# Routed expert rows: scattered into a region per expert and loaded as plain tiles, in place of a token list and row gathers

## The chip, the cores and the metric

The kernel runs on one NeuronCore of a Trainium2 chip. Its engines are TensorE (PE), VectorE (DVE), ScalarE (ACT), GpSimd (POOL) and SyncE (SP); 16 DMA engines move data between HBM and the on-chip SBUF. The metric is the time of one execution on the device, in microseconds, as a median of several runs.

## The reference

The tokens are 16 batches of 128 rows, 2048 in all, of 256 floats. Four blocks with a residual follow each other: a convolution block, a low-rank expert layer, a cross attention, and a mixture of experts. All but the last are computed per batch and aren't touched. The last one:

```python
logits = flat @ router_w.T                      # 2048 x 32
scores = jnp.sqrt(jax.nn.softplus(logits))
_, idx = jax.lax.top_k(scores + expert_bias, 4)
topv = jnp.take_along_axis(scores, idx, axis=1)
topv = topv / (topv.sum(axis=-1, keepdims=True) + 1e-20)
out = sum(p_e[:, None] * swiglu(flat, wg_e, wu_e, wd_e) for e in range(32)) + swiglu(flat, shared...)
x = x + out
```

Each token goes to 4 of 32 experts; an expert has an inner width of 128, and gate and up are clipped to [-7, 7].

## The kernel before

The five engines have one program each, written out by hand. Up to the routed experts the order on an engine is set by a table of ticks: for each engine and kind of step the tick of the first instance (T_PE, T_DVE, T_ACT, T_POOL), and the program goes through all ticks and emits what is due. A batch comes every 128 ticks; a tick has no time of its own, it only orders an engine's instructions. Engines wait for each other by semaphores.

The normalized rows of a batch (xnD, ScalarE) are written by SyncE to the HBM tensor xn_rows (L1367). Routing is done in five groups of batches. For each group VectorE ranks the tokens of every expert and computes a key per token and rank (the four picks of a token, k = 0 to 3, sorted by expert number). GpSimd then scatters the token's number into token_list in HBM, one indirect DMA of 128 pieces of 4 bytes for each batch and rank, 64 in all (L1310); the list has 2048 places for each expert.

Behind the ticks, when the shared expert's 16 steps are done, the list is turned into tiles of 128 rows: SyncE loads it (L1392), TensorE transposes it and selects with one-hot matrices (L552 to L563), VectorE builds those (L925 to L951). The result is idg, the token numbers of 95 tiles (the most that 8192 picks on 32 experts can need), and regs, each tile's weight address. GpSimd gathers the rows of each tile from xn_rows by indirect DMA (L1322) into 32 buffers xg.

The tile loop is a software pipeline of NT + 6 steps. In step t TensorE makes the down product of tile t-5 (L580, out of bank y), transposes tile t (L594, L595), transposes the activated tile t-4 (L598) and makes gate and up of tile t-1 (L606, with weight addresses from registers that it loads for 16 tiles at a time). ScalarE copies the transposed rows (L1222), takes the tanh (L1217) and copies the result into one of four buffers y (L1227). VectorE clips, multiplies and copies (L972, L974, L984, L980), and computes beside it each token's places in y_rows and its weights pk4. SyncE writes each result tile to y_rows (L1396) and counts those that have landed in s_st.

At the end the results are gathered back by token: for each rank, from 3 to 0, and each batch one indirect DMA on GpSimd (L1340) into the same ring xg, then one multiply-add on VectorE into xs (L1062), then the output is written (L1403). A rank's gathers wait for s_st to reach the last tile with such a pick (register thr). y_rows is filled with zeros at the start (L1361), since places without a token may be read.

## Time and profile before

| | us |
|---|---|
| median of 3 runs | 824.38 (823.39 to 824.93) |
| the profiled execution | 827.63 |
| its span, first to last instruction | 825.8 |

| engine | busy us | share |
|---|---|---|
| TensorE matmuls | 608.2 | 74% |
| VectorE | 508.2 | 62% |
| GpSimd | 443.7 | 54% |
| ScalarE | 357.4 | 43% |

The mean granted clock of TensorE is 0.868. Times in the profile are counted from the first instruction. An idle time has behind its arrow what ended it by the trace; "issue" means that the profile shows nothing that the engine waited for, and "remote" an update for which it has no source.

### The profile page before, as it was taken

How to read it: one execution, taken by the hardware profiler on the slowest of the kernel's cores; microseconds unless marked ns; L12 is line 12 of the kernel's file. 1: busy time of each engine (PE TensorE's matmuls, PEld its weight loads, DVE VectorE, ACT ScalarE, POOL GpSimd, SP SyncE). 2: the span in 40 equal slices, each digit the busy share in tenths (PEclk: the TensorE clock that was granted, in tenths of full speed). 3: DMA queues.
4: the chain of work that ended last, by engine and by line, in shares of the span. 5: the costliest groups of instructions: out<-in, count | busy, mean ns of one | idle time of the engine just before them, and what ended most of it. 6: DMA issues, size and time to landing. Idle time of an engine off the chain costs nothing.

```text
span 825.8 us, 13944 instructions
## 1 busy us (share of the span) xinstructions
PE 608.2 (74%) x4063; PEld 485.0 (59%) x4063; DVE 508.2 (62%) x1582; ACT 357.4 (43%) x1012; POOL 443.7 (54%) x592
## 2 busy tenths in 40 slices
PE   0779999999799996998787347741689999678200
PEld 0678777878678785786564136631467777456100
DVE  1537767677976679756773545610388788546733
ACT  1012566567465674657955423210245544334100
POOL 6687573646437885226412473177355552535675
PEclk9999999999799997999877556875699999989655
DMA  7893000000000000007302070033244443335236
GB/s 289 309 349 111 1 8 8 1 8 8 8 8 1 9 8 7 8 2 267 129 7 84 1 273 14 8 113 103 89 138 153 154 145 116 108 96 152 65 108 180
DMA packets 51386, 75.29 MB, mean 91 GB/s; under 512 B 7249, under 2 KB 40529, under 8 KB 51057
## 3 DMA queue, kind: packets, MB, share of 16 engines
q1 hardware_dynamic: 41552, 53.25, 18.4%
q0 software_dynamic: 9760, 21.15, 9.3%
q8 instruction: 35, 0.57, 0.3%
q14 instruction: 39, 0.31, 0.1%
HBM read 44.98 MB, written 29.39 MB: 90 GB/s over the span
## 4 chain that ended last, share of the span: by engine, by line
PE 57%; DVE 15%; issue 11%; another core or an unknown queue 6%; ACT 5%; POOL 3%; DMA 2%; SPq 1%; POOLq 0%; ACTq 0%; DVEq 0%
PE pc L542 10%; PE ps L606 9%; PE pS L580 5%; PE pS L522 4%; PE ps L508 3%; PE ps L338 3%; PE po L493 2%; POOL work L1340 2%; PE ps L378 2%; PE ps L365 2%; PE ps L382 2%; PE ps L399 1%; PE ps L391 1%; DMA arena<-in_ctxT 1%
## 5 line engine op out<-in xcount | busy, mean ns | idle before, releaser
L1322 POOL DMA_INDIRECT work<-xn_rows,tk x95 | 92.1, 969 | 88.3 <-issue 39.7
L542 PE MATMUL pc<-arena,tk 128*128 128x128 f32 x768 | 105.5, 291 | 15.2 <-POOL arena L1298 9.3
L542 PEld LDWEIGHTS pc<-arena,tk 128*128 128x128 f32 x768 | 98.6, 205 | 18.2 <-issue 9.7
L580 PE MATMUL pS<-arena,tk 128*128 x190 | 65.4, 427 | 55.7 <-issue 40.6
L606 PE MATMUL ps<-arena,work 128*128 x380 | 103.8, 398 | 0.0
L1340 POOL DMA_INDIRECT work<-y_rows,tk x64 | 71.0, 1110 | 59.0 <-PE pc L595 24.9
L1298 POOL TENSOR_TENSOR arena<-arena 128x512 f32<-128x512 f32 x64 | 90.1, 1426 | 12.4 <-ACT arena L1097 12.3
L1217 ACT ACTIVATE tk<-work 128x128 f32<-128x128 f32 x95 | 29.4, 309 | 120.4 <-DVE work L972 81.9
L580 PEld LDWEIGHTS pS<-arena,tk 128*128 128x128 f32 x190 | 29.8, 196 | 80.4 <-issue 80.1
L1162 ACT ACTIVATE work<-pS,work 128x128 f32<-128x128 f32 x256 | 72.7, 373 | 7.8 <-DVE work L787 7.7
L1310 POOL DMA_INDIRECT token_list<-pk,ixl x64 | 63.8, 996 | 22.3 <-issue 15.2
L972 DVE TENSOR_SCALAR work<-ps 128x256 f32<-128x256 f32 x95 | 40.1, 422 | 53.4 <-remote 25.0
L606 PEld LDWEIGHTS ps<-arena,work 128*128 128x128 f32 x380 | 68.6, 201 | 5.9
L1235 POOL TENSOR_TENSOR stD<-stD,epsc 128x1 f32<-128x1 f32 x16 | 3.0, 187 | 106.7 <-DVE stD L619 106.7
L787 DVE TENSOR_REDUCE work<-pS 128x4 f32<-128x512 f32 x64 | 43.8, 685 | 26.5 <-PE pS L522 26.5
L769 DVE TENSOR_TENSOR arena<-pc,arena 128x512 f32<-128x512 f32 x64 | 43.8, 684 | 24.6 <-PE pc L542 24.2
L980 DVE COPY tk<-po 128x128 f32<-128x128 f32 x95 | 27.5, 289 | 43.5 <-issue 16.8
L508 PE MATMUL ps<-pk,work 128*128 128x128 f32 x256 | 44.5, 301 | 8.4 <-ACT work L1162 4.6
L1154 ACT ACTIVATE work<-ps 128x512 f32<-128x512 f32 x64 | 37.8, 591 | 23.0 <-PE ps L508 21.5
L1062 DVE SCALAR_TENSOR_TENSOR xs<-work,pk,xs 128x256 f32<-128x256 f32 x64 | 28.1, 478 | 26.6 <-DMA work<-y_rows,tk 24.0
L522 PE MATMUL pS<-arena,work 32*128 32x256 f32 x256 | 40.0, 433 | 0.3
L508 PEld LDWEIGHTS ps<-pk,work 128*128 128x128 f32 x256 | 30.6, 152 | 16.1 <-issue 15.5
(288 smaller groups left out, 1443.7 us busy)
## 6 DMA issues: line engine op xcount, KB each, us to landing
arena<-in_w SPq DMA_DIRECT2D x8, 1536.0 KB
y_rows<-lg SPq DMA_DIRECT2D x1, 12160.0 KB, 38.6
y_rows<-tk SPq DMA_DIRECT2D x95, 128.0 KB
tk<-in_tk SPq DMA_DIRECT2D x1, 2048.0 KB, 10.9
xn_rows<-xnD SPq DMA_DIRECT2D x16, 128.0 KB
out<-xs SPq DMA_DIRECT2D x16, 128.0 KB
pk<-in_pack SPq DMA_DIRECT2D x1, 1588.0 KB, 11.6
xs<-in_x SPq DMA_DIRECT2D x3, 512.0 KB, 11.6
```

Source lines behind the costliest of these rows:

```text
L508: i = pe.transpose(p[:, 128 * k:128 * k + 128], Pt[m % 3][:, 128 * k:128 * k + 128], ident)
L522: i = pe.matmul(p[:, 256 * c:256 * c + 256], qT[b % 3][r, 128 * c:128 * c + 128], kz[b % 3][r, c, :, :].rearrange("p a b -> p (a b)"), sta ...
L542: i = pe.matmul(pv, tk[:, h, 128 * d:128 * d + 128], kvv[:, ci, :, :].rearrange("p b (i h j) -> p (b i) h j", i=8, h=8)[:, :, hl, :], star ...
L580: pe.matmul(p[:, 0:256], hT[n % 2], arena[:, 512:][:, bass.ds(base.pop(n), 256)], start=True, stop=True).then_inc(s_yp, 1)
L606: i = pe.matmul(p[:, 0:256], xgT[n % 3][:, 128 * c:128 * c + 128], arena[:, 256 * c:][:, bass.ds(base[n], 256)], start=(c == 0), stop=(c = ...
L769: dve.tensor_tensor(zv, cbanks.place["conv", n][:, :].rearrange("p (k h j) -> p k h j", h=4, j=8), x1, ALU.mult).then_inc(s_z, 1)
L787: dve.tensor_reduce(mx[:, g, :], sbanks.place["S", m][:, :].rearrange("p (k m) -> p k m", k=4), AX.X, ALU.max, negate=True).then_inc(s_mx, 1)
L1162: i = act.activation(Pt[m % 3][:, 128 * k:128 * k + 128], sbanks.place["S", m][:, 128 * k:128 * k + 128], ACT.Exp, bias=mx[:, g, k:k + 1])
L1298: pool.tensor_tensor(kv[kk % 4][:, c, half, :].rearrange("p (i h j) -> p i h j", h=8, i=8), i0, i1, ALU.mult).then_inc(s_kv, 1)
L1310: pool.indirect_dma_start(out=Ld, out_offset=bass.IndirectOffsetOnAxis(ap=ixl[:, b, k:k + 1], axis=0), in_=P("tok")[:, b:b + 1], in_offset ...
L1322: pool.indirect_dma_start(out=xg[n % NX], out_offset=None, in_=Xd, in_offset=bass.IndirectOffsetOnAxis(ap=idg[:, n:n + 1], axis=0)).then_i ...
L1340: pool.indirect_dma_start(out=xg[n % NX], out_offset=None, in_=Yd, in_offset=bass.IndirectOffsetOnAxis(ap=ixy[:, b, k:k + 1], axis=0)).the ...
```

## The change

The regions that the token list had become regions of rows. The key of a pick, minus one, is now directly a row of the HBM tensor expert_rows, with 2048 rows for each expert and 512 more, each 272 floats: 256 of data, then the number of its place in y_rows. At the start SyncE writes the places' numbers into xn_rows, which now has four copies of each token (one per rank), and fills all 32 regions with padding rows, whose place is one of 512 dump rows. ScalarE writes the normalized rows, four copies, and takes over SyncE's weight and row loads. For each batch and rank SyncE loads 128 rows into one of four staging buffers, and GpSimd scatters them by the key.

The list load, its transposes and selections go. A tile is a plain load of 128 rows from an address in a register (12 buffers in place of 32, four loads in flight), computed from the experts' counts in a few small steps beside the shared expert (ta to te). GpSimd scatters each result tile to y_rows by the places that came with the rows, and the results are read back as plain loads of four batches at a time into four buffers of their own. The weight extraction in the loop moves from step 44 to step 6 on, the threshold computation changes. The ticks have new values throughout; those of GpSimd and the new ones of SyncE are shown.

```diff
-NT = 95
+U = 128
+Q = 128 // U
+NT = -(-((NB * 128 * KT + NE * (U - 1)) // U) // Q)
+ROW = 272
-NX = 32
+DUMP = 512
+NX = 12
-        xg = [carve([128, 256]) for _ in range(NX)]
+        xg = [carve([128, 260]) for _ in range(NX)]
+        rb = [carve([128, 4, 256]) for _ in range(4)]
-        T_POOL = {"rsA": 70, "rsB": 680, "rsC": 818, "rsD": 1153, "vc": 269, "us": 405, "kv": 279, "xb": 699,
-            "xc": 1050, "list": 1914}
+        T_POOL = {"rsA": 84, "rsB": 684, "rsC": 812, "rsD": 1148, "vc": 297, "us": 337, "kv": 273, "xb": 801,
+            "xc": 1117, "list": 1899}
+        T_SP = {"fill": 1162, "st": 1855}
...
@@ tensor_program, the tile loop
-                    pe.wait_ge(d_g[n % 8], 16 * (n // 8 + 1))
+                    pe.wait_ge(d_g[n % 4], 16 * Q * (n // 4 + 1))
@@ vector_program, the end
-                dve.scalar_tensor_tensor(out=xs[:, b, :], in0=xg[n % NX], scalar=pk4[:, b, k:k + 1], in1=xs[:, b, :],
-                                         op0=ALU.mult, op1=ALU.add).then_inc(s_fin, 1)
+            for m in range(4 * KT):
+                g, k = m % 4, KT - 1 - m // 4
+                dve.wait_ge(d_r[g], 16 * (m // 4 + 1))
+                for i in range(4):
+                    b = 4 * g + i
...
+                    dve.scalar_tensor_tensor(out=xs[:, b, :], in0=rb[g][:, i, :], scalar=pk4[:, b, k:k + 1], in1=xs[:, b, :],
+                                             op0=ALU.mult, op1=ALU.add).then_inc(s_fin, 1)
@@ scalar_program
+                for b in at(t, T_ACT["xd"], 128, NB):
+                    act.wait_ge(s_xn["D"], b + 1)
+                    act.dma_start(Xd[:, 128 * b:128 * b + 128, 0:256].rearrange("k p d -> p k d"),
+                                  xnD[b % 2][:, :].unsqueeze(1).broadcast_to((128, KT, 256))).then_inc(d_xn[b % 2], 16)
@@ gpsimd_program
+                        j = KT * b + k
                         pool.wait_ge(s_ixl, g + 1)
+                        pool.wait_ge(d_st[j % 4], 16 * (j // 4 + 1))
                         pool.indirect_dma_start(
-                            out=Ld, out_offset=bass.IndirectOffsetOnAxis(ap=ixl[:, b, k:k + 1], axis=0),
-                            in_=P("tok")[:, b:b + 1], in_offset=None).then_inc(d_list, 16)
...
+                            out=Xs, out_offset=bass.IndirectOffsetOnAxis(ap=ixl[:, b, k:k + 1], axis=0),
+                            in_=stage[:, j % 4, :], in_offset=None).then_inc(d_list[j % 4], 16)
+
+            for n in range(NT + 3):
+                if n >= 3:
+                    pool.wait_ge(d_y[(n - 3) % 4], 16 * ((n - 3) // 4 + 1))
+                    pool.sem_inc(s_st, 1)
+                if n < NT:
+                    pool.wait_ge(s_y, n + 1)
+                    pool.indirect_dma_start(
+                        out=Yr, out_offset=bass.IndirectOffsetOnAxis(ap=xg[n % NX][:, 256:257].bitcast(U32), axis=0),
+                        in_=y[n % 4], in_offset=None).then_inc(d_y[n % 4], 16)
@@ sync_program
+            for t in range(TICKS):
+                for e in (*at(t, 0, 1, 14), *(14 + n for n in at(t, T_SP["fill"], 36, NE - 14))):
+                    sp.dma_start(Xs[e * NB * 128:(e + 1) * NB * 128, :].rearrange("(j p) d -> p j d", p=128),
+                                 stage[:, e % 4, :].unsqueeze(1).broadcast_to((128, NB, ROW))).then_inc(d_zero, 16)
...
+                        if j == 0:
+                            sp.wait_ge(d_zero, 16 * (NE + 2))
+                        if k == 0:
+                            sp.wait_ge(d_xn[b % 2], 16 * (b // 2 + 1))
+                        if j >= 4:
+                            sp.wait_ge(d_list[j % 4], 16 * (j // 4))
+                        sp.dma_start(stage[:, j % 4, :], Xd[k, 128 * b:128 * b + 128, :]).then_inc(d_st[j % 4], 16)
+            sp.wait_ge(s_regs, 1)
...
+                if n >= 4:
+                    sp.wait_ge(d_g[n % 4], 16 * Q * (n // 4))
+                if n >= NX:
+                    sp.wait_ge(d_y[(n - NX) % 4], 16 * ((n - NX) // 4 + 1))
+                for k in range(Q):
+                    r = sp.snap(half[Q * n % WR + k], min_val=0, max_val=NE * NB * 128 + 384)
+                    sp.dma_start(xg[n % NX][U * k:U * k + U, :], Xs[bass.ds(r, U), 0:260]).then_inc(d_g[n % 4], 16)
...
+            for m in range(4 * KT):
+                g, k = m % 4, KT - 1 - m // 4
+                if g == 0:
+                    sp.wait_ge(s_st, last[k])
+                    sp.sem_inc(s_thr, 1)
+                if m >= 4:
+                    sp.wait_ge(s_fin, 4 * (m - 4) + 4)
+                o = DUMP + NB * 128 * k + 512 * g
+                sp.dma_start(rb[g], Yr[o:o + 512, :].rearrange("(b p) d -> p b d", p=128)).then_inc(d_r[g], 16)
```

Three places show the order of instructions. First SyncE from the last input loads on, before (lg is a block of zeros, xnD the normalized rows, in_w the experts' weights):

```order
L1361 DMA y_rows<-lg 128x95x256
L1367 DMA xn_rows<-xnD 128x256 x11
L1378 DMA arena<-in_w 128x4x768 x5
L1367 DMA xn_rows<-xnD 128x256 x3
L1370 DMA tk<-in_w 128x768
```

And after (in_dest holds the places' numbers, in_pad the padding rows):

```order
L1339 DMA xn_rows<-in_dest 8192x16
L1341 DMA stage<-in_pad 128x1088
L1343 DMA expert_rows<-stage 128x4x272
L1347 DMA expert_rows<-stage 128x16x272 x32
L1359 DMA stage<-xn_rows 128x272 x64
```

The writes of rows and the loads of weights have left SyncE's queue, and 64 staging loads stand behind 32 region fills.

Second GpSimd, where the first group's scatters begin. After (st... are the statistics of the layer norms, L1296 the products for the convolution):

```order
L1303 TENSOR_TENSOR xs<-xs,rows 128x256
L1296 TENSOR_TENSOR arena<-arena 128x512
L1310 DMA expert_rows<-stage,ixl 66048x272
L1296 TENSOR_TENSOR arena<-arena 128x512
L1310 DMA expert_rows<-stage,ixl 66048x272
L1236 TENSOR_TENSOR stD<-stD,epsc 128x1
L1238 TENSOR_TENSOR stD<-stD,nhalf 128x1
L1240 TENSOR_SCALAR stD<-stD 128x1
```

The scatters stand among the statistics and the products, as the list scatters did, but each now stands behind a wait for its staging load.

Third the end of GpSimd's program, before:

```order
L1235 TENSOR_TENSOR stD<-stD,epsc 128x1
L1237 TENSOR_TENSOR stD<-stD,nhalf 128x1
L1239 TENSOR_SCALAR stD<-stD 128x1
L1310 DMA token_list<-pk,ixl 65536x1 x23
L1322 DMA work<-xn_rows,tk 128x256 x95
L1328 TENSOR_LOAD thr
L1329 ISA
L1340 DMA work<-y_rows,tk 128x256 x64
```

And after:

```order
L1236 TENSOR_TENSOR stD<-stD,epsc 128x1
L1238 TENSOR_TENSOR stD<-stD,nhalf 128x1
L1240 TENSOR_SCALAR stD<-stD 128x1
L1310 DMA expert_rows<-stage,ixl 66048x272 x22
L1320 DMA y_rows<-tk,work 8704x256 x95
```

Both sets of gathers, 95 and 64, are gone from GpSimd, and 95 scatters of results have come.

## Rows read from the trace of the kernel before

**Rows 1.** Stages: busy time and count of each engine, clock, DMA share.
```profile
core 0: us, PE busy (x) PEld busy (x) DVE busy (x) ACT busy (x) POOL busy (x), PEclk, DMA share, GB/s
...
60.00:380.00 320.00, 295.76 (x2365) 245.27 (x2364) 232.80 (x660) 187.50 (x519) 181.18 (x286) 0.97 0.05 16
...
528.00:590.00 62.00, 20.28 (x74) 14.47 (x73) 11.16 (x43) 6.19 (x19) 37.65 (x40) 0.61 0.29 87
590.00:708.00 118.00, 114.36 (x589) 88.27 (x588) 94.49 (x336) 57.45 (x195) 54.44 (x56) 0.99 0.44 136
708.00:770.00 62.00, 45.51 (x216) 34.03 (x214) 31.71 (x111) 21.51 (x72) 30.34 (x32) 0.92 0.41 124
770.00:825.80 55.80, 0.04 (x1) 0.00 (x0) 27.10 (x62) 0.38 (x1) 40.69 (x32) 0.51 0.41 117
```

**Rows 2.** Timeline of GpSimd, 533 to 582: start, duration, operation, idle before.
```profile
533.75 0.98 POOL L1322 DMA_INDIRECT work<-xn_rows,tk  x1 [23.78 <-DVE tk L949]
535.04 0.96 POOL L1322 DMA_INDIRECT work<-xn_rows,tk  x1 [0.30 <-issue]
...
581.36 0.95 POOL L1322 DMA_INDIRECT work<-xn_rows,tk  x1 [0.30 <-issue]
```

**Rows 3.** Timeline of ScalarE: copies of transposed tiles 0, 6, 8 and later.
```profile
537.30 0.38 ACT L1222 ACTIVATE work<-ps 128x256 f32<-128x256 f32 x1 [8.52 <-PE ps L595]
...
577.39 0.38 ACT L1222 ACTIVATE work<-ps 128x256 f32<-128x256 f32 x1 [10.39 <-remote]
...
590.99 0.38 ACT L1222 ACTIVATE work<-ps 128x256 f32<-128x256 f32 x1 [0.89 <-PE ps L595]
...
597.32 0.36 ACT L1222 ACTIVATE work<-pc 128x256 f32<-128x256 f32 x1
...
598.98 0.36 ACT L1222 ACTIVATE work<-ps 128x256 f32<-128x256 f32 x1
...
633.51 0.36 ACT L1222 ACTIVATE work<-pc 128x256 f32<-128x256 f32 x1
...
635.82 0.38 ACT L1222 ACTIVATE work<-ps 128x256 f32<-128x256 f32 x1 [0.55 <-PE ps L595]
...
712.60 0.36 ACT L1222 ACTIVATE work<-pc 128x256 f32<-128x256 f32 x1
...
762.87 0.36 ACT L1222 ACTIVATE work<-ps 128x256 f32<-128x256 f32 x1
```

**Rows 4.** Timeline of TensorE in the first tiles of the loop.
```profile
558.11 1.22 PE L580 MATMUL pS<-arena,tk 128*128 x2 [10.28 <-issue]
...
582.14 1.22 PE L580 MATMUL pS<-arena,tk 128*128 x2 [20.47 <-issue]
```

**Rows 5.** Waits, 484 to 500 us: total, times, longest.
```profile
ACT pk L1184 <- remote: 9.7, 1, 9.7
```

**Rows 6.** Timelines of VectorE and GpSimd in the tail.
```profile
769.02 13.56 DVE L1062 SCALAR_TENSOR_TENSOR xs<-work,pk,xs 128x256 f32<-128x256 f32 x34
...
823.21 0.48 DVE L1062 SCALAR_TENSOR_TENSOR xs<-work,pk,xs 128x256 f32<-128x256 f32 x1 [0.94 <-DMA work<-y_rows,tk]
...
773.01 10.39 POOL L1340 DMA_INDIRECT work<-y_rows,tk  x1 [0.30 <-DVE xs L1062]
```

**Rows 7.** Stages again: y_rows written in 1 KB rows, then weights read.
```profile
45.00:50.00 5.00, 3.97 (x32) 3.72 (x32) 1.21 (x3) 0.60 (x1) 4.90 (x6) 1.00 1.05 348
382.00:396.00 14.00, 11.44 (x95) 8.17 (x92) 10.17 (x33) 11.39 (x35) 9.90 (x14) 1.00 1.03 403
```

**Rows 8.** The list tensor: durations min/median/max in ns, first and last start.
```profile
L1310 POOL DMA_INDIRECT token_list<-pk,ixl x64: 954/976/1113, 264.2 to 508.9; - x64
```

**Rows 9.** VectorE, TensorE and the chain between shared expert and first tile.
```profile
528.09 0.17 DVE L631 TENSOR_SCALAR tk<-cum 128x32 f32<-128x32 f32 x1
...
536.57 0.48 PE L594 MATMUL ps<-pk,work 128*128 128x128 f32 x1 [2.37 <-DMA work<-xn_rows,tk]
...
535.04 2.67 DMA work<-xn_rows,tk
```

424 lines of the change are left out of this document (177 added, 247 removed), and 9 rows, old and new, of tables (T_ACT, T_DVE, T_PE).

## The prediction

> **What bounds the kernel now.** I read the stages first: busy time of each engine from 60 us on [rows 1]. Until 380 us TensorE is busy 295.76 of 320 us and the DMA engines 5%: a compute stage with an almost idle memory side. From 590 to 708 us, the plain run of the expert tiles, TensorE is busy 114.36 of 118 us. Between and behind them lie three stretches where nothing is busy that should be: 528 to 590 (TensorE 20.28 of 62 us), 708 to 770 (45.51 of 62) and 770 to the end (none of 55.8 us).
>
> The first hole begins when GpSimd starts its row gathers. They go out back to back, one each 1.25 us (533.75, 535.04, ... 581.36), because 32 tile buffers are free [rows 2]. The loop advances only slowly meanwhile: ScalarE copies the transposed rows of tile 0 at 537.30, of tile 6 at 577.39, of tile 8 at 590.99 [rows 3]. TensorE stands still for 10.28 and 20.47 us "by issue", with no DMA named [rows 4]. Once GpSimd is throttled by the buffers, one gather per tile, the loop runs: tile 8 at 590.99, tile 74 at 712.60 are 1.84 us a tile, and a plain step, 597.32 to 598.98, is 1.66 us [rows 3]. The same pattern stands at the other bursts: while 16 list scatters leave back to back, ScalarE waits 9.7 us for an update no row accounts for [rows 5]. I read this as: a long back-to-back burst of indirect DMAs on GpSimd delays the updates TensorE sends to others. The trace shows the coincidence, not the cause.
>
> The tail: VectorE is through the loop at 769.02, runs 34 accumulations in 13.56 us, and the remaining ones come at the pace of GpSimd's gathers until 823.21; the span ends at 825.8 [rows 6].
>
> **Part by part; the sum is made on the profiled execution** (827.63 us, span 825.8), whose time lies 3.25 us above the median of the three runs; differences are applied to that median, 824.38.
>
> *Fill of the regions.* SyncE writes 32 regions of 2048 rows of 1088 B, 71.3 MB, from SBUF, where the kernel before writes 12.45 MB. Plain writes of 1024 B rows ran at 348 GB/s with all DMA engines busy (1.05), and descriptors of 3 KB at 403 GB/s [rows 7]. Per row that is 46.8 ns and 122 ns of an engine, so about 9 ns fixed and 0.037 ns per byte; 1088 B take 49.1 ns, and 65,536 of them on 16 engines 201 us. The fill can start when the loads are through and the pad rows sit in SBUF, at 38 to 47 us by my estimate (loads of 8.7 MB at 300 to 400 GB/s, then 8192 pieces of 64 B for the token numbers). During it ScalarE issues seven or eight fourfold writes of the normalized rows, 0.5 MB each, some 1.5 us of all engines apiece: 11 us. So it ends between 250 and 260 us, or about 280 if the token numbers take long or an odd row size costs a little. The cover is the compute stage, DMA share 0.05 [rows 1]. Who waits: SyncE holds the first staging load until all fills have landed, GpSimd's first scatter waits for that load, and behind it in GpSimd's order stand the rstd steps and the products for the convolution, for which TensorE waits. The first list scatter of before left at 264.2 us [rows 8]; a staging load needs some 2.7 us [rows 9]. So a loss of 0 to 20 us; I take +5.
>
> *Scatter of rows instead of a list.* 64 scatters on GpSimd either way, 1 us each. Now each needs a staging load through four buffers. A round of load (about 2.7 us), scatter (1 us) and landing (2.7 us) is 6.4 us per four, 1.6 us each in place of 1.26. At the end 22 stand in a row, 35 us from 474: through at 509 to 515, and they are needed only when the shared expert is done at 528. Covered; without that cover it would be some 8 us. What a late staging load costs GpSimd's other work in the compute stage is bounded by one round, 0 to 6 us, and I count it inside the +5.
>
> *Index tables.* Out goes the chain list load, transposes, two selections, gather: from 528.09 on VectorE to the first transposed tile at 536.57, 8.5 us [rows 9]. In come some 25 small VectorE operations of 0.17 to 0.2 us beside the shared expert, where VectorE is nearly the bound: +4.5. Behind the last shared step remain two transposes, two casts, a register load, one DMA: 0.5+0.5+0.65+0.3+2.7 = 4.7 us, -3.8; the register load is read off the step at 633.51, which has one on TensorE and lasts 2.31 us for 1.66 [rows 3]. Together +0.7.
>
> *The loop.* Gathers leave GpSimd, plain loads on SyncE take their place (12 buffers, four in flight); GpSimd now scatters each result, one per tile, at 0.95 to 1.25 us under a step of at least 1.66. It can never burst: each scatter waits for its own result. So the hole from 528 to 590 should go, and with it the burst at 709 and its hole. ScalarE's copies of tile 0 and tile 94 are 225.6 us apart now (537.30, 762.87) [rows 3]. 94 steps cost 156 us at the plain step and 173 at 1.84; the one-hot work of before on 512-wide tiles in the loop is dropped, the weight extraction stays, so I take 1.78, 167.3 us: -58.3. The reuse of a tile buffer closes in time: result of tile n written at step n+5, scatter and landing some 4 us, load 3 us, is under ten steps of twelve.
>
> *The tail.* 64 gathers become 16 loads of 512 KB that do not wait for tile buffers. Of the 95 tiles 79 hold tokens in these inputs, and the four ranks are complete after tile 67, 74, 77 and 79 (counted from the reference's routing), so all are ready before the loop ends; but only four read buffers exist, so most of the reading runs beside VectorE. 64 accumulations at 13.56/34 = 0.40 us are 25.6 us, +2 for late loads (512 KB at 348 GB/s 1.5 us against 1.6 us of work per group), +2.6 for the last output (823.21 to 825.8), +2 for GpSimd to drain: 32 us, where 56.8 stand now [rows 6]: -24.8. Bounds: 28 with perfect reads, 56.8 if reading is as slow as gathers.
>
> What GpSimd does under VectorE's run is visible: the gather issued at 773.01 took 10.39 us, not 0.95, while VectorE ran its 34 accumulations [rows 6]. The last two or three scatters of the new loop meet 64 of them; they carry padding tiles, so no read waits for them, only the end of the program does. The Trainium skill, "SBUF — State Buffer", section on who interferes with whom, says that VectorE and GpSimd share a port pair as an exclusive lock and that descriptor writing on GpSimd starves meanwhile, and asks for the plain queues; the trace agrees in kind. By that rule the drain would come wholly after VectorE's last operation, 3 x 1.25 + 2.7 = 6.5 us instead of 2.6+2, a sum 2 us higher.
>
> **Sum:** +5 +0.7 -58.3 -24.8 = -77.4; 824.4 - 77.4 = **747 us**.
>
> **Rivals.** *The fill is late.* The rows are 1088 B, a multiple of 64 but not of the usual powers, while the price above is from 1024 B rows. If each costs 56 ns, the fill takes 230 us, ends at 290 and GpSimd is held 20 to 40 us in the compute stage: about 775. For it: the estimate ends within 10 us of the need, and nothing in the trace has such a row. Against: even 280 costs little. The Trainium skill, "DMA: Bandwidth & Descriptors", section "How a descriptor splits into AXI transactions", states that a piece not starting on 256 B is split further and fetches unused bytes: up to 40 beats in place of 34, which gives the 56 ns by the same fit; no row here shows it. Chance 0.17.
>
> *The holes stay.* If the silence of TensorE's updates hangs on something other than the burst (say, on any indirect DMA beside it at the loop's start), 40 to 50 us of the gain fail: about 793. Against: from 590 to 708 GpSimd issues one per tile and nothing stalls [rows 1, 3]. 0.12.
>
> *Slower than before.* The loop's step becomes the scatter's. GpSimd allows three result scatters in flight and waits for the one three tiles back before it issues the next; four result buffers stand behind ScalarE's copy. If a 128-row scatter to HBM needs L us to land beside the tile loads, the step is about (L+1)/3. From 1.78 to 2.6 us a tile costs 94 x 0.82 = 77 us and eats all the gain; that needs L of 7 us, against 2.67 for a gather [rows 9]. At 3 us a tile: 860 us. 0.05.
>
> *Better than that.* The paced row scatters no longer hold up the routing stage, where 9.7 us and some smaller waits sit on the chain [rows 5]: about 733. 0.2.
>
> **How the numbers follow.** My forecast has 0.46 (735 to 762), the better case 0.2, the late fill 0.17, the holes 0.12, slower 0.05. To leave out no more than two in ten the range goes from 722 (better case with clean steps of 1.66 us) to 788 (late fill with all of its 40 us). A change of under 0.2%, some 1.6 us, is about what this measurement cannot tell from none; hardly any case ends there. Faster 0.94, same 0.01, slower 0.05.
>
> **What would show it.** Right: DMA share near 1 from about 40 to 250 us with the convolution running at its old pace; GpSimd's first row scatter near 265; no idle TensorE of over 3 us inside the loop; 1.7 to 1.85 us between ScalarE's copies throughout; VectorE's 64 accumulations in under 30 us, end 3 to 7 us later. Wrong: GpSimd waiting at its first scatter well past 275 while TensorE idles; TensorE idle "by issue" near the first tiles; ScalarE's copy of a result waiting for the scatter's landing; VectorE waiting for each read group.

## The result, and the profile after

The changed kernel takes **782.29 us** (median of 4 runs, 781.09 to 783.03), the kernel before 824.52 in the same comparison; the ratio is 0.9488 (95% interval 0.9472 to 0.9505). The forecast was 747, range 722 to 788: right in direction and inside the range, but the gain is 42.2 us and not 77.4. A second measurement of the same kernel, beside e9, gave 777.98 us (e10), so some 4 us lie between comparisons.

The profiled execution has a span of 781.2 us (before 825.8). The DMA row of its page, in 40 slices of 19.5 us:

```profile
DMA  8999999999999433101343924952344343434669
```

It stands at 8 or 9 up to the 13th slice, 254 us: the fill. Stages, with the columns of [rows 1]:

```profile
core 0: us, PE busy (x) PEld busy (x) DVE busy (x) ACT busy (x) POOL busy (x), PEclk, DMA share, GB/s
60.00:380.00 320.00, 286.14 (x2286) 237.63 (x2286) 237.39 (x632) 182.64 (x499) 174.24 (x274) 0.96 0.74 236
528.00:554.00 26.00, 2.78 (x13) 1.51 (x11) 2.76 (x10) 0.79 (x3) 6.73 (x7) 0.59 0.27 83
554.00:743.00 189.00, 170.09 (x835) 133.36 (x834) 123.19 (x433) 81.75 (x277) 85.90 (x88) 0.93 0.44 134
743.00:781.20 38.20, 5.28 (x22) 3.04 (x20) 29.29 (x77) 2.98 (x10) 10.87 (x7) 0.61 0.80 264
```

Against [rows 1], the long standstill at the loop's start is gone, and so is the slow tail. But from 528 to 554 TensorE is again busy for only 2.78 us, before the loop has begun, and inside the loop it is idle for 19 us, of which no forecast of mine had more than a few.

**Where the loop starts.** The timeline of SyncE's queue and of ScalarE, and the total of GpSimd's row scatters (durations min/median/max in ns, first and last start; then what it waited for):

```profile
550.88 7.12 SPq L1376 DMA_DIRECT2D work<-expert_rows  x12
```

```profile
553.83 0.38 ACT L1223 ACTIVATE work<-ps 128x256 f32<-128x256 f32 x1 [24.97 <-PE ps L593]
```

```profile
L1310 POOL DMA_INDIRECT expert_rows<-stage,ixl x64: 957/963/1192, 267.9 to 548.2; - x64
its engine sat idle before it (us, times) until:
  DMA stage<-xn_rows: 41.8, 11
```

Tile 0 is copied at 553.83, where [rows 3] had 537.30 and the forecast comes to 543. The first tile load waits for the last scatter, issued at 548.2 and not at 509 to 515. GpSimd waited 41.8 us for its four staging buffers to be loaded. The last scatters, in its timeline:

```profile
528.48 0.96 POOL L1310 DMA_INDIRECT expert_rows<-stage,ixl  x1 [6.28 <-DMA stage<-xn_rows]
529.75 0.96 POOL L1310 DMA_INDIRECT expert_rows<-stage,ixl  x1 [0.30 <-issue]
535.03 0.96 POOL L1310 DMA_INDIRECT expert_rows<-stage,ixl  x1 [4.33 <-DMA stage<-xn_rows]
536.30 0.96 POOL L1310 DMA_INDIRECT expert_rows<-stage,ixl  x1 [0.31 <-issue]
541.63 0.96 POOL L1310 DMA_INDIRECT expert_rows<-stage,ixl  x1 [4.37 <-DMA stage<-xn_rows]
```

They come in pairs, 6.6 us apart: 3.3 us a scatter, where I had put 1.6. SyncE issues the last staging loads in pairs too:

```profile
532.18 0.80 SPq L1359 DMA_DIRECT2D stage<-xn_rows  x2
538.73 0.79 SPq L1359 DMA_DIRECT2D stage<-xn_rows  x2
545.34 0.32 SPq L1359 DMA_DIRECT2D stage<-xn_rows  x1
```

Each of these stands 2.4 us behind the second scatter of a pair (529.75, 536.30, 542.89), at its landing. The reason is the order. The buffer of scatter j is j % 4. Group 3 (batches 12 to 14) has 12 scatters at ticks 16 apart from 1408 on, group 4 (batch 15) four from 1536 on, so the last four of group 3 and the four of group 4 stand at the same ticks, and both engines take them in turn: 56, 60, 57, 61, 58, 62, 59, 63. Their buffers are 0, 0, 1, 1, 2, 2, 3, 3. Every second load needs the buffer of the scatter just ahead of it and waits for that scatter to land.

**Inside the loop.** Copies of tiles 15, 16 and 17 on ScalarE, and TensorE between the first two:

```profile
579.03 0.37 ACT L1223 ACTIVATE work<-pc 128x256 f32<-128x256 f32 x1
584.10 0.38 ACT L1223 ACTIVATE work<-ps 128x256 f32<-128x256 f32 x1 [3.68 <-PE ps L593]
587.09 0.38 ACT L1223 ACTIVATE work<-pc 128x256 f32<-128x256 f32 x1 [0.44 <-PE pc L593]
```

```profile
583.09 0.69 PE L577 MATMUL pS<-arena,tk 128*128 x2 [3.61 <-issue]
```

Most steps take 1.66 us or alternate between 1.47 and 2.10. The steps into tile 16, 32, 48, 64 and 80 take 5.07, 5.07, 5.90, 5.96 and 5.43, and each of them is followed by one of 2.6 to 3.2. These are the places at which TensorE loads 16 registers with expert bases. The loads, in before and in after:

```profile
L572 PEldq TENSOR_LOAD <-regs x6: 1257/1313/1789, 534.5 to 733.2; - x6
```

```profile
L568 PEldq TENSOR_LOAD <-regs x6: 4112/4298/4533, 531.0 to 712.1; - x6
L1366 SPq TENSOR_LOAD <-regs x6: 977/1170/1481, 545.7 to 705.4; - x6
```

The same 16 words cost TensorE 1.31 us before and 4.30 after, while SyncE loads 16 words of the same row in 1.17 (medians).

**The tail** is as forecast; VectorE from the end of the loop on:

```profile
749.48 8.00 DVE L1040 SCALAR_TENSOR_TENSOR xs<-work,pk,xs 128x256 f32<-128x256 f32 x20
757.79 16.29 DVE L1040 SCALAR_TENSOR_TENSOR xs<-work,pk,xs 128x256 f32<-128x256 f32 x40 [0.32 <-DMA work<-y_rows]
775.41 1.67 DVE L1040 SCALAR_TENSOR_TENSOR xs<-work,pk,xs 128x256 f32<-128x256 f32 x4 [1.33 <-DMA work<-y_rows]
```

64 accumulations are through at 777.1; from 749.3 to the span's end are 31.9 us, against 32 forecast and 56.8 before [rows 6].

The account of the two spans, measured between ScalarE's copies of tile 0 and tile 94 (742.91): start +16.5, loop 189.1 in place of 225.6 = -36.5, from tile 94 to the end 38.3 in place of 62.9 = -24.6; together -44.6. That is the difference of the two profiled spans; the medians differ by 42.2.

### The profile page after: what moved, and what is told of

Read it like the earlier page. It is cut to its first block, busy times and chain, and to the rows that moved or that the text cites. A ratio compares the mean times of both kernels' runs of the same rounds, so it can differ in the third digit from the quotient of the medians.

```text
span 781.2 us, 14111 instructions
## 1 busy us (share of the span) xinstructions
PE 600.9 (77%) x4045; PEld 480.6 (62%) x4045; DVE 511.7 (65%) x1554; ACT 356.5 (46%) x1010; POOL 376.5 (48%) x526
## 4 chain that ended last, share of the span: by engine, by line
PE 31%; SPq 29%; DMA 14%; issue 10%; DVE 8%; POOL 4%; ACT 3%; ACTq 0%; DVEq 0%; POOLq 0%
SPq L1347 26%; PE ps L605 8%; PE pS L577 5%; DMA stage<-xn_rows 3%; DMA expert_rows<-stage,ixl 3%; DMA expert_rows<-stage 3%; PE pc L556 2%; POOL y_rows L1320 2%; DMA stage<-in_pad 2%; DMA y_rows<-tk,work 2%; SPq L1330 2%; DVE xs L1040 2%; PE ps L522 2%; PE pS L536 2%; DMA work<-y_rows 1%
## 5 line engine op out<-in xcount | busy, mean ns | idle before, releaser
L1320 POOL DMA_INDIRECT y_rows<-tk,work x95 | 96.8, 1019 | 112.4 <-ACT tk L1228 95.0
L556 PEld LDWEIGHTS pc<-arena,tk 128*128 128x128 f32 x768 | 97.6, 203 | 19.8 <-DVE arena L773 13.3
L1296 POOL TENSOR_TENSOR arena<-arena 128x512 f32<-128x512 f32 x64 | 89.8, 1420 | 11.1 <-ACT arena L1101 11.0
L1310 POOL DMA_INDIRECT expert_rows<-stage,ixl x64 | 63.9, 998 | 59.0 <-DMA stage<-xn_rows 41.8
L1223 ACT ACTIVATE work<-ps 128x256 f32<-128x256 f32 x48 | 17.9, 373 | 45.9 <-PE ps L593 44.5
L1228 ACT ACTIVATE tk<-pS 128x256 f32<-128x256 f32 x95 | 35.8, 377 | 5.0 <-DMA y_rows<-tk,work 5.0
L536 PE MATMUL pS<-arena,work 32*128 32x256 f32 x256 | 37.2, 408 | 0.7 <-ACT work L1151 0.7
## 6 DMA issues: line engine op xcount, KB each, us to landing
arena<-in_w ACTq DMA_DIRECT2D x8, 1536.0 KB, 13.3
```

Source lines behind the costliest of these rows:

```text
L536: i = pe.matmul(p[:, 256 * c:256 * c + 256], qT[b % 3][r, 128 * c:128 * c + 128], kz[b % 3][r, c, :, :].rearrange("p a b -> p (a b)"), sta ...
L556: i = pe.matmul(pv, tk[:, h, 128 * d:128 * d + 128], kvv[:, ci, :, :].rearrange("p b (i h j) -> p (b i) h j", i=8, h=8)[:, :, hl, :], star ...
L1296: pool.tensor_tensor(kv[kk % 4][:, c, half, :].rearrange("p (i h j) -> p i h j", h=8, i=8), i0, i1, ALU.mult).then_inc(s_kv, 1)
L1310: pool.indirect_dma_start(out=Xs, out_offset=bass.IndirectOffsetOnAxis(ap=ixl[:, b, k:k + 1], axis=0), in_=stage[:, j % 4, :], in_offset=N ...
L1320: pool.indirect_dma_start(out=Yr, out_offset=bass.IndirectOffsetOnAxis(ap=xg[n % NX][:, 256:257].bitcast(U32), axis=0), in_=y[n % 4], in_o ...
```

## The experiments

There were five comparisons; e1 to e4, e5 to e8, e9 to e11 and e12 ran on four different chips. The kernel before took 824.5 us in the first comparison, 822.5 beside e1 to e4, 749.8 beside e5 to e8, 822.8 beside e9 to e11 and 749.3 beside e12. Program and inputs are the same in all; what the chip changes is the subject of e5 and e9 to e11. After itself was measured in the first comparison (782.3) and in e10 (778.0) only, so a gain given below against 782.3 could be up to 4 us smaller.

### The register table's place (e1, e2, e7)

In before the table is one row of 96 words, and TensorE loads 16 from each multiple of 16. In after it is 190 words: 95 row addresses for SyncE, then 95 bases for TensorE, so that TensorE's groups start at word 95 + 16 m, 60 bytes behind a multiple of 64 bytes. (Offsets here are counted from the start of the row; where the row itself lies in SBUF is not on record.) e1 changes that:

```diff
-        regs = sb("regs", [1, 2 * Q * NT], I32)
+        regs = sb("regs", [1, 192], I32)
-                    pe.load(half[:w], regs[0:1, Q * (NT + t):Q * (NT + t) + w])
+                    pe.load(half[:w], regs[0:1, 96 + t:96 + t + w])
```

(VectorE's two copies into the table go to words 0 and 96 accordingly. What lies behind the table in SBUF moves by 8 bytes.)

> The changed kernel with nothing altered but where the second half of the register table lies: the expert bases that TensorE loads start at word 96 of the table's row instead of word 95, so that each group of 16 starts at a multiple of 64 bytes again, as it did in the kernel before. In the trace of after TensorE's load of 16 registers takes 4298 ns, in that of before 1313 ns, and the step from tile 15 to 16 (and 31 to 32, 47 to 48, 63 to 64, 79 to 80) takes 5.1 to 5.9 us where a plain one takes 1.66. Theory (the misaligned start makes the load slow): the load is back at 1.2 to 1.8 us, the five steps fall to some 2.3 us, and with the steps at the lower clock behind them 15 to 22 us go: 760 to 767 us. Rival (SyncE's load of its own 16 registers from the same row at about the same time gets in the way): both loads still fall together, TensorE's stays at 4.1 to 4.5 us and the time within 1 us of after's 782.3.

Measured: **754.55 us**, 0.9161 of before (0.9127 to 0.9195). The register loads of e1:

```profile
L568 PEldq TENSOR_LOAD <-regs x6: 1104/1284/1598, 526.9 to 686.3; - x6
L1366 SPq TENSOR_LOAD <-regs x6: 977/1166/1554, 541.4 to 679.4; - x6
```

TensorE's load is fast, and the rival is out. It was a weak one: in both kernels SyncE's second load stands over 7 us ahead of TensorE's (570.2 and 577.9 in after, 566.1 and 573.5 in e1), so they never ran at the same time. The step into tile 16 is 1.84 us (from 574.67) and the one behind it 2.10:

```profile
576.51 0.39 ACT L1223 ACTIVATE work<-ps 128x256 f32<-128x256 f32 x1 [0.45 <-PE ps L593]
578.61 0.37 ACT L1223 ACTIVATE work<-pc 128x256 f32<-128x256 f32 x1
```

The loop's 94 steps take 163.5 us instead of 189.1. That is 25.6 us for one word of padding (23.4 against the 186.9 of e10), more than the 15 to 22 expected: a load of 4.3 us costs the step it stands in 3 to 4 us and the next ones 1 to 2 more. Behind the idle stretch of after the granted clock is down, as the stages (TensorE alone) from 578 us show, its column being the one behind the count:

```profile
578.00:583.00 5.00, 1.48 (x9) 1.00 0.50 158
583.00:587.00 4.00, 3.91 (x14) 0.64 0.20 66
```

e2 makes the opposite edit in the kernel before:

```diff
-        regs = sb("regs", [1, 96], I32)
+        regs = sb("regs", [1, 127], I32)[:, 31:127]
```

> The kernel before, with its register table moved by 31 words, so that each group of 16 registers that TensorE loads starts 60 bytes behind a multiple of 64, as in the changed kernel; SyncE loads nothing there. Theory (alignment): the load goes from 1.31 to 4.1 to 4.5 us, five of them stand in the loop, each adds 3 us and some steps at the lower clock: 838 to 845 us instead of 824.5. Rival (two engines loading at once): one engine loads alone here, 1.3 us each, 824 to 825.5 us.

Measured: 843.95 us, 1.0233 (1.0182 to 1.0284), with one engine loading, as expected; its loop takes 241.7 us where that of before takes 225.6:

```profile
L572 PEldq TENSOR_LOAD <-regs x6: 3938/4176/4302, 532.6 to 747.8; - x6
```

e7 exchanges the two halves in after, so that SyncE has the odd start:

```diff
-                    pe.load(half[:w], regs[0:1, Q * (NT + t):Q * (NT + t) + w])
+                    pe.load(half[:w], regs[0:1, t:t + w])
-                    sp.load(half[:w], regs[0:1, Q * n:Q * n + w])
+                    sp.load(half[:w], regs[0:1, NT + n:NT + n + w])
```

(VectorE's two copies change places accordingly, and SyncE waits for both. The table keeps its 190 words, so nothing else in SBUF moves.)

> The changed kernel with the two halves of the register table exchanged: TensorE's expert bases lie at word 0 (each 16 at a multiple of 64 bytes), SyncE's row addresses at word 95 (60 bytes behind one). Theory (alignment decides, whichever engine loads): SyncE's load goes from 1.17 to about 4 us, TensorE's from 4.3 to 1.3; SyncE issues its loads up to 12 tiles ahead, so its 3 us are covered, and the time is near that of the aligned table, 752 to 758 us. Rival (only TensorE's load suffers from the odd start): SyncE's load stays at 1.0 to 1.5 us, same time.

Measured: 756.36 us (one run). The loads of e7:

```profile
L568 PEldq TENSOR_LOAD <-regs x6: 1219/1383/1633, 529.2 to 690.0; - x6
L1366 SPq TENSOR_LOAD <-regs x6: 3442/3806/3908, 545.1 to 683.0; - x6
```

The slow load follows the odd start to SyncE, and its 3.8 us cost nothing there, since SyncE issues tile loads well ahead. The loop takes 163.5 us again. So the start in the row decides, on either engine. Only an offset of 60 bytes was tried; which offsets are slow is open. The Trainium skill, "Runtime: NRT & Kernel Launch", section "Instruction fetch mechanics", puts register loads at about 200 ns a register, for loads that by the same page come from HBM; for 16 that would be 3.2 us, an estimate. The loads here come from SBUF, and these traces have 82 ns a register at an aligned start (1313/16) and 269 at the odd one, so one figure doesn't cover them.

### The ring of staging buffers (e3, e4, e8, e12)

e3 has eight staging buffers from the 37th scatter on. One of the four new ones is a fifth slice of the old tile; the others are the tiles that held the normalised rows of three earlier stages, free since 444 us:

```diff
+        slots = [stage[:, i, :] for i in range(5)] + [xnABC[:, i, :] for i in range(3)]
+        slot = [j % 4 if j < 36 else j % 8 for j in range(KT * NB)]
+        turn = [slot[:j].count(slot[j]) for j in range(KT * NB)]
...
-                        if j >= 4:
-                            sp.wait_ge(d_list[j % 4], 16 * (j // 4))
-                        sp.dma_start(stage[:, j % 4, :], Xd[k, 128 * b:128 * b + 128, :]).then_inc(d_st[j % 4], 16)
+                        s, c = left[slot[j]]
+                        if turn[j]:
+                            sp.wait_ge(s, c + 16 * turn[j])
...
+                        sp.dma_start(slots[slot[j]], Xd[k, 128 * b:128 * b + 128, :]).then_inc(loaded[slot[j]][0], 16)
```

> The changed kernel with eight buffers for the rows on their way to the scatters instead of four, from the 37th scatter on (a fifth buffer, and the three tiles of normalised rows of earlier stages, free by then). Nothing else moves; the scatters and loads are the same 64 and 64. Theory (the ring of four sets the pace: a load waits for the scatter four places before it, 4.4 us of landing and 2 to 7 us of load for each round): the last 18 scatters go at 1.3 to 1.7 us each instead of 3.2, the last one by 518 to 528 us instead of 548.2, the first tile's copy by 530 to 536 instead of 553.8, and the time falls by 17 to 23 us: 759 to 765 us. Rival (the expert weights that land in the same stretch slow every transfer, so more of them at once only wait longer): the scatters' pace stays above 2.5 us, 776 to 782 us.

Measured: 763.98 us, 0.9284 (0.9247 to 0.9322), as the theory had it. The scatters of e3:

```profile
L1315 POOL DMA_INDIRECT expert_rows<-stage,ixl x52: 956/985/1225, 268.3 to 525.6; - x52
L1315 POOL DMA_INDIRECT expert_rows<-xnABC,ixl x12: 956/959/966, 472.6 to 526.8; - x12
```

The last of all is issued at 526.85 instead of 548.20. The pace was not quite the expected 1.3 to 1.7 us: the last 15 scatters (from 498.14) stand 2.05 us apart on average, the last seven (from 518.97) 1.3.

This edit changes two things at once. There are twice the buffers, and with j % 8 the last eight scatters, 56, 60, 57, 61 and so on, have the buffers 0, 4, 1, 5, 2, 6, 3, 7: none is taken twice in a row. No run has four buffers in an order without such pairs, so it isn't shown how much of the gain needs the other four. By after's trace the pairs are the larger part: the last seven steps took 27.0 us (521.25 to 548.20), and at the forecast's 1.6 us they would have taken 11.2. That is an estimate.

The first tile's copy came at 539.35, later than the 530 to 536 expected, and SyncE's waits from 480 to 560 us show why:

```profile
SPq L1376 <- DVE regs L958: 16.9, 1, 16.9
```

L1376 is SyncE's load of its row addresses. With the scatters early, the register table is what SyncE waits for: it is written at 533.9 in e3, since its transposes stand behind the shared expert's last product on TensorE. (Right behind the row of seven scatters VectorE and ScalarE wait there for updates without a source, 2.95 and 3.93 us until 529.0: a small standstill of the kind that before has.) e4 joins both remedies:

> The aligned register table and the eight buffers together. If both theories hold and the two costs lie one behind the other (one before the loop's first tile, one inside the loop), the gains add: 738 to 748 us, and the loop's 94 steps take 165 to 175 us instead of 189. If the loop's steps at the lower clock have another cause than the loads, the loop stays above 178 us and the time above 750.

Measured: **742.71 us**, 0.9005 (0.8953 to 0.9057); the loop takes 165.7 us, tile 0 is copied at 536.12. Against after's trace (553.83 and 189.1) that is 17.7 at the start and 23.4 in the loop, so each cost lies where it was thought to be. The gain of 39.6 is less than the 27.7 of e1 and the 18.3 of e3 together; 4.4 of e1's lay at the start (549.48), which its edit doesn't touch, and all three are counted from the 782.3 of another comparison.

e8 moves the table ahead of the last shared-expert blocks, by two entries of the tick tables:

```diff
-            "S": 971, "tab": 3371, "conv": 404, "oP": 1124}
+            "S": 971, "tab": 3325, "conv": 404, "oP": 1124}
-            "tb": 3243, "tc": 3288, "td": 3293, "te": 3422}
+            "tb": 3243, "tc": 3288, "td": 3293, "te": 3330}
```

> Aligned table, eight buffers, and beside these the register table's two transposes on TensorE and its two copies on VectorE placed three shared-expert blocks earlier. In the run with both remedies SyncE's first tile load is issued at 531.75 us, right behind the table's copies (about 531), though the last scatter was issued at 525.21. Theory (the table is then the last thing that the first tile load waits for): the load goes out at 527.5 to 529, tile 0 is copied at 532 to 534 instead of 536.1, and the time is 738 to 741 against 742.7. Rival (the shared expert's end on TensorE at about 531 sets the start by itself): tile 0 at 535 to 536.5 and 741.5 to 744.

Measured: **733.59 us** (5 runs), below the expected 738 to 741. The first load goes out at 525.26 (expected 527.5 to 529) and tile 0 is copied at 530.05 (expected 532 to 534). Part of the 9 us against e4 may be the chip's, as e4 was not run there. The edit's own part can be read from ScalarE's last normalised rows to its copy of tile 0: 48.9 us in e4 (487.24 to 536.12), 45.3 in e8 (484.80 to 530.05) and 45.6 in e12 (487.11 to 532.66), so some 3.5 us. But on that chip the kernel before takes 749.76, so e8 stands at 0.9782 (0.9764 to 0.98) of it only. e12 is the same version once more:

> The version with aligned table, eight buffers and early table once more, on whatever chip this call gets; its first run was on the chip where the kernel before takes 750 us. Theory (it keeps GpSimd's rows of indirect DMAs short of a standstill nearly everywhere, so that it is the same on both kinds of chip): 733 to 741 us, so 0.89 to 0.90 of before if before takes 822 here, with at most one standstill of some 6 us, between 490 and 500 us, where up to nine scatters stand in a row. Rival (the eight buffers make rows long enough for a full standstill there): over 745 us.

Measured: 733.95 us against 749.3 for before, 0.9776 (0.975 to 0.9801). It was again a chip of the faster kind, so what e8's version takes on one of the other kind was not measured; e4's 0.9005 is the nearest.

### The standstills of the kernel before (e5, e9, e10, e11)

The prediction's largest term was that TensorE's standstills come from long rows of indirect DMAs on GpSimd. e5 shortens the row in before: at most 8 tiles ahead instead of 32.

```diff
-                if n >= NX:
-                    pool.wait_ge(s_gP, n - NX + 1)
+                if n >= 8:
+                    pool.wait_ge(s_gP, n - 7)
```

> The kernel before, with GpSimd's gathers of the loop held to at most 8 tiles ahead of TensorE's transposes, where it could be 32 ahead; buffers, gathers and their order stay. In the trace of before 32 gathers run in a row from 533.75 to about 581, one each 1.25 us, and in the same stretch the steps from tile 4 to 7 take 10.8, 22.5 and 11.3 us. Theory of the prediction (the uninterrupted row of gathers makes the holes; they go with it): the three steps fall to 2 to 3 us each, some 38 us go, 783 to 790 us. Rival (the holes belong to something else at the start of the loop, such as weights or code being fetched): the three steps stay above 9 us and the time is 822 to 828. A third: the gather's own landing is too slow for 8 ahead, and the loop gets a wait of another kind: above 828.

Measured: 764.34 us, where before itself took 749.76: 1.0185 (1.0154 to 1.0216). None of the three expectations had that. In e5's trace the loop has no standstill at all: tile 0 at 519.92, tile 94 at 685.52, 165.6 us. In its tail the 64 gathers of results then start only at 674.1, run in a row at 1.25 us each until 756.7, and the end waits for GpSimd; that is what being only 8 ahead costs. If one takes the trace of before and replaces its first copy (537.30) by 519.92 and its loop (225.6) by 165.6, the span is 748.4, which is the 747.0 to 750.6 that the runs of before have here. So on this chip the kernel before seems to run without standstills, though no profile of it was taken there. The wait of [rows 5] is gone too: from the last normalised rows to the shared expert's last operation e5 takes 40.5 us, before 54.2 and after 43.3. e9 to e11 ran together on another chip.

> The kernel before, unchanged, with a profile of its own. On the chip of the last call its median was 749.8 us, on the two chips of the calls ahead of that 824.5 and 822.5, each with a spread under 0.7%. Theory (the standstills of TensorE near 485 to 497, 544 to 588 and at tiles 75 to 77 appear on some chips and not on others, with the same program and inputs): either the time is 820 to 827 us with a loop of some 225 us and the three standstills, or 747 to 753 us with a first tile at 519 to 521 us and a loop of 164 to 167 us without them, and nothing between. Rival (the standstills come and go with small shifts in time, on any chip): times between 760 and 815 us, or one of the standstills without the others.

Measured: 822.91 us, a first copy at 534.76, a loop of 224.8 and the standstills in their old places. Time and trace match one of the two patterns. ScalarE's copies of tiles 4 to 7 in e9, and below them tiles 75 to 77:

```profile
542.44 0.37 ACT L1222 ACTIVATE work<-ps 128x256 f32<-128x256 f32 x1
548.62 0.39 ACT L1222 ACTIVATE work<-pc 128x256 f32<-128x256 f32 x1 [2.70 <-remote]
568.24 0.39 ACT L1222 ACTIVATE work<-ps 128x256 f32<-128x256 f32 x1 [9.67 <-remote]
585.78 0.39 ACT L1222 ACTIVATE work<-pc 128x256 f32<-128x256 f32 x1 [3.40 <-remote]
...
710.44 0.37 ACT L1222 ACTIVATE work<-pc 128x256 f32<-128x256 f32 x1
717.58 0.39 ACT L1222 ACTIVATE work<-ps 128x256 f32<-128x256 f32 x1 [1.99 <-remote]
726.75 0.39 ACT L1222 ACTIVATE work<-pc 128x256 f32<-128x256 f32 x1
```

> The kernel before with its gathers held to 8 tiles ahead, once more, since on the chip of its first run the kernel before had no standstills to remove; there it was 14.6 us slower, because GpSimd reaches its 64 gathers of results later. Theory (the row of 32 gathers back to back brings out the standstill of 544 to 588 on chips that show it): on a chip where before takes 822 the steps from tile 4 to 7 fall from 44.5 us in all to under 8, and with 14.6 us lost at the end the time is 795 to 802 us. Rival (the row of gathers has nothing to do with it): the three steps stay above 30 us and the time is 835 to 842. On a chip where before takes 750 it is 762 to 767 again and tells nothing more.

Measured on the same chip as e9: 808.32 us, 0.983 (0.9794 to 0.9865), between the two expectations. The steps from tile 4 to 7 fall from 43.3 us in e9 (6.18, 19.62, 17.54) to 12.4 (5.69, 3.61, 3.12). But a standstill turns up where neither before nor e9 had one: the four steps from tile 88 to 92 take 40.4 us, where four plain ones take 6.7. ScalarE's copies there:

```profile
698.10 0.36 ACT L1222 ACTIVATE work<-ps 128x256 f32<-128x256 f32 x1
702.61 0.38 ACT L1222 ACTIVATE work<-pc 128x256 f32<-128x256 f32 x1 [0.63 <-remote]
713.21 0.38 ACT L1222 ACTIVATE work<-ps 128x256 f32<-128x256 f32 x1 [4.81 <-issue]
734.90 0.38 ACT L1222 ACTIVATE work<-pc 128x256 f32<-128x256 f32 x1 [7.56 <-remote]
```

and GpSimd's gathers of results in e11, one each 1.25 us from 696.71 to 730.56:

```profile
696.71 0.94 POOL L1340 DMA_INDIRECT work<-y_rows,tk  x1 [0.40 <-issue]
...
730.56 0.95 POOL L1340 DMA_INDIRECT work<-y_rows,tk  x1 [0.30 <-issue]
735.56 0.94 POOL L1340 DMA_INDIRECT work<-y_rows,tk  x1 [4.05 <-remote]
```

The shortened row at the loop's start lost most of its standstill, and the long row that now stands later has one: the first late copy (702.61) comes 6 us behind the row's start, the last (734.90) 4 us behind its end. In e9 the one at tiles 75 to 77 stands beside the same kind of row (706.84 to 723.13). In e5, the same program on another chip, the same row of 1.25 us steps begins at 674.13 and the copies beside it go on at their pace:

```profile
677.19 0.37 ACT L1222 ACTIVATE work<-pc 128x256 f32<-128x256 f32 x1
678.85 0.37 ACT L1222 ACTIVATE work<-ps 128x256 f32<-128x256 f32 x1
```

So it takes both: a long row of indirect DMAs on GpSimd, and a chip that reacts to it. No chip on record was used in two comparisons, so that it is the chip, and not something else that differed between the comparisons, is the likeliest reading and not shown; what differs in the chips is open as well.

> The changed kernel, unchanged, beside the kernel before on the same chip. Its trace had no such standstills on the chip where before had them, and kernels that differ from it by little ran within 2 us of each other on two chips. Theory (only the kernel before has the standstills, so the worth of the change depends on the chip): 780 to 784 us whichever chip it is; so 0.945 to 0.952 of before where before takes 822, and 1.038 to 1.046 of it, slower, where before takes 750. Rival (the faster chip is faster for every kernel): a ratio near 0.95 on both.

Measured beside e9: 777.98 us, 0.9445 (0.9407 to 0.9482), 2 us under the expected band; no standstill of this kind in its loop, which takes 186.9 us. The theory's band for the other kind of chip and the rival (a ratio near 0.95 on both kinds of chip) could not be tested directly: after itself was not run on a chip of the faster kind. Two kernels close to it were: e7, which has the slow load covered, takes 756.4 us there against 749.8, and e6, below, 772.6. By parts, from the first copies of e5 and e7 (519.9 and 553.1) +33, from the loops (165.6, and 189.1 of after) +23.5, from the tail -24.6: some 32 us more than before, about 782. That is an estimate; that e6, which does less than after, is slower than before there was measured.

### The fill (e6)

```diff
-                    sp.dma_start(Xs[e * NB * 128:(e + 1) * NB * 128, :].rearrange("(j p) d -> p j d", p=128),
-                                 stage[:, e % 4, :].unsqueeze(1).broadcast_to((128, NB, ROW))).then_inc(d_zero, 16)
+                    sp.dma_start(Xs[e * NB * 128:e * NB * 128 + 512, :].rearrange("(j p) d -> p j d", p=128),
+                                 stage[:, e % 4, :].unsqueeze(1).broadcast_to((128, 4, ROW))).then_inc(d_zero, 16)
```

> The changed kernel with only the first 512 rows of each expert's region filled in advance, instead of 2048: 17.8 MB written and not 71.3. Left out is the fill of rows that no token reaches with these inputs (the fullest expert has 499), so the kernel would not be right for others. The prediction put the fill at +5 us, all by the first scatter, which waits for it. Theory (the fill only delays the first scatter, and the index groups behind it catch up): the first scatter runs at 262 to 265 us instead of 267.9, the compute stage up to 440 us gains 0 to 5 us, and the whole 0 to 5: 777 to 782.5. Rival (writing at 350 GB/s beside the compute slows loads and steps there more than the trace shows): 765 to 776 us.

Measured: 772.62 us, beside 749.76 for before (1.03, 1.0268 to 1.0332): 5.4 us under after's 777.98 of e10 and 9.7 under its first 782.29, both from other comparisons. Of that 1.4 us (against e10) or 3.6 (against after) lie in the loop, which the fill doesn't touch. The first scatter hardly moves (266.8 instead of 267.9), so this is not the fill holding up the scatters. The time lies in the band of the rival (765 to 776) and not in the theory's (777 to 782.5), but after was not measured on that chip. What moves is the compute stage. ScalarE's writes of the last normalised rows, first and last start, in before, after and e6:

```profile
L1072 ACT ACTIVATE xnD<-xs,stD x16: 599/600/602, 120.3 to 474.0; 128x256 f32<-128x256 f32 x16
```

```profile
L1050 ACT ACTIVATE xnD<-xs,stD x16: 599/601/607, 119.0 to 487.3; 128x256 f32<-128x256 f32 x16
```

```profile
L1050 ACT ACTIVATE xnD<-xs,stD x16: 599/600/601, 121.0 to 482.5; 128x256 f32<-128x256 f32 x16
```

Before and after are level at the fifth batch (217.57 and 217.53), 6.0 us apart at the eighth and 13.3 at the sixteenth. With a quarter of the fill the sixteenth comes at 482.55. On the same chip, with the whole fill, it came at 487.52 in e7 and 484.80 in e8, and all eight traces with the whole fill lie between 484.53 (e1) and 488.83 (e3). So the fill's share is 2 to 6 us by these, and not well known from one run. The rest, 7 to 11 us, is open: the scatters in GpSimd's order and the changed order of the steps both came with the change, and no run separates them.

## Why the prediction was right or wrong, point by point

The direction was right, and for the reason given. That 782 lies inside the range is partly luck: it is outside the forecast's own band (735 to 762), and the upper end, 788, was drawn for a late fill that didn't come. Two costs that the forecast didn't have, the late scatters and the slow register load, took its place. The comparison also ran on a chip where before has its standstills, as in the profile that the forecast was read from; on the other kind of chip the sign would, by e6, have been wrong.

**Fill: the timing right, its price too low.** The DMA engines are full until 254 us, the last fill landed at 264.85 (forecast: ends at 250 to 260, at 280 at worst), the first scatter stands at 267.9. The late-fill rival fell with it. By the section "How a descriptor splits into AXI transactions" of the Trainium skill, "DMA: Bandwidth & Descriptors", with the most beats for every row, the fill would have ended near 290, an estimate. The trace doesn't agree: rows of 1088 B went at 350 GB/s, as those of 1024 B had [rows 7], which is 49.7 ns a row and an engine, where I had put 49.1 and the rival 56. The price was +5 and the compute stage ended 13.3 us late instead, by the last normalised rows.

**Row scatters: the step that failed at the loop's start.** The prediction's round of load, scatter and landing "is 6.4 us per four". The round was right at the end of the row, and "per four" was wrong. It takes 6.6 us there, but carries two scatters: the last eight come from two groups whose ticks coincide, and take each buffer twice in a row. Both groups and their ticks stand in the kernel. The 14 steps ahead of them (487.54 to 521.25) took 2.4 us each instead of 1.6; there a staging load needed up to 7.5 us until its scatter could start (508.36 to 515.88, and 2.9 at the very end), and three loads of weights, 4.7 MB, were issued at 493 to 495. That they are the reason is not shown. And the row began 13.3 us later than in before. "Covered" was thus false: the shared expert was done at 530.6, and the last scatter was issued at 548.2. e3 removes that for 18.3 us, by more buffers and by another order of them at once.

**Index tables: half of the price right, the place wrong.** SyncE's table was written at about 530.7, directly behind the shared expert's last operations, where the forecast had put it, and was hidden behind the late scatters. With those gone it became what the start waits for. In e3 the stretch from the shared expert's last operation to the copy of tile 0 is 5.6 us (533.79 to 539.35), in before 9.1: -3.6 where -3.8 was forecast. The +4.5 for the small operations on VectorE no run separates. Moving the table ahead was worth some 3.5 us (e8).

The start in sum: +16.5 where +5.7 was forecast (compute stage +13.3; routing and shared expert -10.7, since the wait of [rows 5] went, which e5 doesn't have either; then +13.9 by the scatters).

**Loop: the mechanism right, one cost not seen.** The long standstill went, and the steps between the register loads average the forecast's 1.66 to 1.8. The 94 steps took 189.1 us against 167.3. The difference is the register load, which I had read off before at 0.65 us a time and carried over, though the diff showed the table's new shape `[1, 2 * Q * NT]`, 95 words to a half. e1 has 163.5 us; with that one word right, this term was forecast within 4 us. The holes-stay rival is out, and e11 shows, where before had only shown a coincidence, that the standstill follows the row of indirect DMAs. What I didn't see is that it doesn't come everywhere: e5, the same program as e11, has none. "The better case" (733) named the routing stage's share of that; it came (-10.7) and was used up in front of it.

**Tail: right**, 31.9 for 32. Of the last four scatters, beside VectorE's accumulations, only the last took long, 4.84 us; the three ahead of it took 0.96, 0.96 and 1.21, and none was waited for. The lock that the Trainium skill, "SBUF — State Buffer", section "Who interferes with whom", describes is held for the whole of one instruction, here 0.4 us. The prediction stretched it over the whole run of accumulations, which would have held all four until 777; the trace doesn't bear that out.

**Slower than before** didn't come in the comparison, and not by its mechanism: ScalarE's copies of results waited for a scatter's landing 5.0 us in all, and only from 744.9 us on, at the last tiles. But on the faster kind of chip the sign is, by e6, this one, since there the change has nothing to remove. The late start and the odd table then cost more than the tail gives.

## What to carry to other kernels

Look at where a register load starts in its SBUF row: with groups of 16 words at multiples of 64 bytes it took 1.3 us, with the same groups 60 bytes behind one 4.3, on two engines; a word of padding was worth 23 to 28 us here. Before relying on a ring of buffers, write down which buffer each transfer takes, in the order in which the engine really issues them: where two groups are interleaved and one buffer is taken twice in a row, the overlap is lost there. Here that was 3.3 us a scatter where 1.6 was counted on. And if a large part of a gain is the removal of standstills that no row explains, measure the kernel before on a second and third chip first: this change is worth 5% on one kind and, by e6 and the estimate beside e10, costs 3 to 4% on the other, while with its flaws mended it is ahead on both (e4 0.90, e8 0.98).

## What the runs showed of the hardware that I had not expected

- 16 registers from one row of SBUF: medians of 1.26 to 1.38 us on TensorE at an aligned start, 4.18 to 4.42 at the odd one; on SyncE 1.17 and 3.81.
- A long row of indirect DMAs on GpSimd, one each 1.25 us, goes with steps of up to 22.5 us for a loop tile (plain: 1.66) in three of five comparisons (824.5, 822.5 and 822.8 us for the kernel before). In the two others, on other chips, that same program takes 749.8 and 749.3, and the like row in e5 stops nothing. 73 us lie between the kinds, and runs of before on one chip lie within 7.
- Rows of 1088 B are written to HBM at 350 GB/s.
